# Key norms by statistics of two heads at a time, routing unrolled and staggered, self attention scored in quarters of the array

## The chip, the cores and the metric

The kernel runs on 1 core of one Trainium2 chip. The metric is the device time of one execution in microseconds (us), as the median of several runs. The hand-written program sets the order of work on each engine: TensorE (PE, with its weight loads PEld), VectorE (DVE), ScalarE (ACT), GpSimd (POOL) and SyncE (SP, whose queue issues DMAs). Engines meet at semaphores only.

## The reference

2,048 rows x of width 256 (64 batches of 32) go through six residual steps, each on layer-normed rows, with float32 throughout:

```
x = x + cross attention 0(norm(x), ctx)        16 heads, ctx 64 x 257 x 128
x = x + self attention(norm(x))                16 heads of 16, within each batch of 32 rows
x = x + experts(norm(x))                       64 experts, 8 of them per row, 64 places each
x = x + cross attention 1(norm(x), ctx)        16 heads of 128, RMS norm of queries and keys
x = x + self attention in fp4 weights(norm(x))
x = x + dense experts(norm(x))                 8 experts, 2 weighted
```

The change touches the second and third step, and a part of the fourth that is computed early. That part is the norm of the keys: for each of 16,448 context rows and each of 16 heads, 1/sqrt(mean of the 128 squared keys + 1e-5), where keys = ctx @ Wk:

```
k = (encoder_hidden_states @ Wk).reshape(B, Skv, H, D)
var = jnp.mean(jnp.square(k), axis=-1, keepdims=True);  rsqrt(var + EPS)
```

The third step gives each row its 8 best experts. An expert takes the first 64 rows that chose it (CAP = 64); what comes later goes nowhere and adds zero:

```
pos = (jnp.cumsum(onehot, axis=0) * onehot).sum(-1) - 1
dest = jnp.where(pos < CAP, slot_expert * CAP + pos, E * CAP)
slot_out = yb[dest] * topk_w      # row E * CAP of yb is zero
```

16,384 choices meet 64 x 64 = 4,096 places.

## The kernel before

x lies in SBUF as 16 tiles of 128 rows (NT = 16). Stages follow each other with a full meeting of all engines between them (`block`): begin, cross_attention 0, self_attention (prefix sa), route (rt), experts (ex), combine (cb), cross_attention 1, self_attention_fp4, dense_experts.

**Key norms** (class KeyNorms, used by rt, ex and cb with their own prefix). The context stands transposed in ctxT, 128 x 16,448: 128 chunks of 128 columns and a rest of 64. A chunk times Wk (128 x 2048) gives four PSUM banks of 512 keys (`keys`, L231, matmul L236; four heads to a bank). Three of the four are squared by ACT into SBUF (L268) and summed per head by DVE (tensor_reduce L295); the fourth is done by ACT alone, four squares with accumulation (L264). Every group of four chunks ACT takes roots (take_root, L275), DVE inverts (L303), PE turns (L243), DVE keeps (L309), and a DMA writes four copies to rk in DRAM. POOL copies the group's piece of ctxT to a staging tile first (put, L225), which the matmuls read. Chunks are shared out as rt 64 (4 a tile), ex 16, cb 48 and the rest.

**self_attention** (L915) is pipelined over tiles, two to a loop turn. Per tile PE turns xn (L972), projects queries and keys (L980) and values (L987), scores (L995), mixes (L1005) and projects out (L1012). k_heads holds the keys masked per head by POOL (L1206), so a score matmul gives 128 queries against 4 heads x 128 keys (all four batches of the tile against each other), four matmuls of 512 columns, though only the 32 x 32 blocks on the diagonal count. ACT picks those (keep_blocks, own_scores, L907, four pieces), DVE subtracts the maximum (L1132, L1133), ACT takes exp (L1074), DVE sums and divides (L1137, L1139) and transposes the blocks in four pieces into probsT (L1144). DVE adds the bias (L1148) and the result (L1150) to x. The mix waits until the add of the tile before is done, since out and mix share a PSUM bank.

**route** (L1224) is a loop of 8 turns of two tiles. Within a tile n PE does keys(0), logits (L1296), keys(1), keys(2), then waits until DVE has chosen the 8 best (L1365 to L1369), counts places (L1303, L1304), keys(3), the turning of the next tile's xn (L1285) and the group's norms (L243). DVE makes codes and places (L1379 to L1387) and the weights (8 operations at L1391, one per choice). POOL scatters the tile's rows with 8 indirect DMAs to slot_rows in DRAM (L1430). The router, Wk and the zeroing of slot_rows are DMAs at the start of the stage.

**experts** (L1437) takes two experts to a turn, 32 turns: rows turned (L1517), gate and up (L1526), hidden turned (L1533), out (L1540); stages lag by 1 and 2 turns. It has two banks for key norms (banks=2) and a chunk in every second turn. A turn's rows and weights come by four DMAs into a ring of 8, the first issued at the stage's start.

**combine** (L1614) takes a tile and a head to a turn, 16 turns in two loop turns of 8. POOL copies the tile's 8 places (L1771) and gathers with 8 indirect DMAs of 128 rows x 1 KB from slot_out (L1776) into one of two buffers got; DVE adds them with their weights (L1746). In between PE folds one head of cross attention 1's weights (turn_head L1668 to L1670, fold_head L1677, L1678; they wait for a load of Wq, Wv and Wo, issued at the start of the stage) and does three chunks of key norms.

```
                    for step, (j, slot, c) in enumerate(chunks(i, t)):
                        norms.keys(pe, j, slot, c)
                        if c == norms.U - 1:
                            norms.turn(pe, j)
                        if step == 0:
                            turn_head(h, t)
                    fold_head(h, t)
```

## Time and profile before

| | |
|---|---|
| median of 3 runs | 3160.76 us (3156.6 to 3161.11) |
| the profiled execution, its own time | 3129.82 us |
| its span on the core | 3128.2 us |
| mean granted TensorE clock | 0.965 |
| busy: PE / DVE / ACT / POOL | 90% / 51% / 46% / 24% |
| self_attention, span's us | 580.66 to 804.95 |
| route | 804.95 to 1121.06 |
| experts | 1121.06 to 1266.77 |
| combine | 1266.77 to 1536.19 |

The stages' limits are the times at which engines leave the meeting between two blocks. A stage's row of windows gives its length, the busy time of each engine in it, PE's mean granted clock and the DMA engines' busy share. PE's sum of busy times counts overlapping matmuls twice, so the starts of matmuls on the timeline tell more of a period than the busy share does.

### The profile page before, as it was taken

What the parts mean: (1) busy time and instruction counts of PE and PEld (TensorE: products, weight loads), DVE (VectorE), ACT (ScalarE), POOL (GpSimd) and SP (SyncE); (2) the same over time, 40 slices, a digit from 0 to 9 for tenths busy, and PEclk for the clock granted to TensorE, in tenths of its full rate; (3) what the DMA queues carried; (4) which work ended last, traced back from release to release, by engine and by line L of the source; (5) the groups of instructions that cost most, each with busy time, mean ns of one, the idle gap of its engine ahead of it and who ended that gap; (6) DMA issues with size and microseconds to landing.
All of it is one profiled execution on the core that took longest, in us unless ns stands there. A gap on an engine that the chain in (4) does not pass through costs nothing. (4 is left out here: it accounts for less than half of the span.)

```text
span 3128.2 us, 53136 instructions
## 1 busy us (share of the span) xinstructions
PE 2826.5 (90%) x13847; PEld 2100.0 (67%) x13847; DVE 1585.7 (51%) x4931; ACT 1436.8 (46%) x4275; POOL 738.0 (24%) x966
## 2 busy tenths in 40 slices
PE   6999999799788869689799999999589999997999
PEld 5888888676443434244367777777478888885888
DVE  3665556467577745477455555555123333332333
ACT  2555455444577756366355555554122223221333
POOL 1332223233345421465221112221310000000000
PEclk8999999899899989799899999999789999998999
DMA  4100000000210066467322222222730000000000
GB/s 150 29 27 23 20 23 13 16 0 0 99 34 7 7 162 192 132 77 74 52 75 74 74 74 74 74 65 63 169 76 0 0 0 0 0 0 27 7 10 10
DMA packets 174812, 157.10 MB, mean 50 GB/s; under 512 B 30315, under 2 KB 158184, under 8 KB 173570
## 3 DMA queue, kind: packets, MB, share of 16 engines
q1 hardware_dynamic: 153922, 130.12, 15.1%
q0 software_dynamic: 13824, 25.23, 5.3%
q10 hardware_dynamic: 6976, 0.75, 0.2%
q8 instruction: 32, 0.52, 0.1%
q14 instruction: 58, 0.48, 0.1%
HBM read 136.89 MB, written 31.67 MB: 54 GB/s over the span
## 5 line engine op out<-in xcount | busy, mean ns | idle before, releaser
L480 PE MATMUL xa_score_ps<-cross_ctxT,xa_qT 128*128 (+1 forms) x1024 | 307.9, 387 | 7.4 <-DVE xa_shift L724 4.1
L500 PE MATMUL xa_mix_ps<-xa_probsT,xa_keys 128*128 128x256 f32 x1024 | 304.2, 380 | 0.0
L236 PE MATMUL rt_kn_key_ps<-moe_wk,rt_kn_stage 128*128 128x512 f32 x512 | 238.7, 608 | 35.4 <-ACT rt_kn_squares L268 18.1
L470 PE MATMUL xa_misc_ps<-xa_xnT,cross_folded 128*128 128x256 f32 x1024 | 234.0, 383 | 6.2 <-ACT xa_squares L593 5.6
L509 PE MATMUL xa_misc_ps<-cross_folded,xa_mixT 128*128 128x256 f32 x1024 | 228.2, 379 | 0.0
L616 ACT ACTIVATE xa_probsT<-xa_probsT_ps 128x256 f32<-128x256 f32 x512 | 188.0, 369 | 79.4 <-PE xa_probsT_ps L487 78.9
L470 PEld LDWEIGHTS xa_misc_ps<-xa_xnT,cross_folded 128*128 128x128 f32 x1024 | 195.6, 192 | 40.0 <-ACT xa_squares L593 12.2
L487 PE MATMUL xa_probsT_ps<-all_ident,xa_probs 128*128 128x128 f32 x1024 | 198.4, 275 | 19.4 <-ACT xa_probsT L616 11.2
L509 PEld LDWEIGHTS xa_misc_ps<-cross_folded,xa_mixT 128*128 128x128 f32 x1024 | 194.6, 190 | 26.5
L236 PE MATMUL cb_kn_key_ps<-moe_wk,cb_kn_stage 128*128 128x512 f32 (+1 forms) x392 | 189.7, 633 | 22.1 <-POOL cb_kn_stage L225 10.2
L736 DVE TENSOR_SCALAR xa_probs<-xa_probs,xa_share 128x257 f32<-128x257 f32 x512 | 199.1, 389 | 18.2
L500 PEld LDWEIGHTS xa_mix_ps<-xa_probsT,xa_keys 128*128 128x128 f32 x1024 | 189.5, 190 | 24.0
L608 ACT ACTIVATE xa_probs<-xa_probs,xa_shift,xa_row_scale 128x257 f32<-128x257 f32 x256 | 153.7, 600 | 108.2 <-DVE xa_shift L724 103.0
L236 PEld LDWEIGHTS rt_kn_key_ps<-moe_wk,rt_kn_stage 128*128 128x128 f32 x512 | 92.3, 191 | 150.0 <-issue 85.6
L487 PEld LDWEIGHTS xa_probsT_ps<-all_ident,xa_probs 128*128 128x128 f32 x1024 | 133.6, 141 | 87.4 <-DVE xa_probs L736 27.9
L608 ACT ACTIVATE xa_probs<-xa_probs,xa_top 128x257 f32<-128x257 f32 x256 | 130.0, 508 | 106.9 <-DVE xa_top L720 104.9
L480 PEld LDWEIGHTS xa_score_ps<-cross_ctxT,xa_qT 128*128 128x128 f32 x1024 | 158.9, 190 | 22.6 <-DVE xa_shift L724 12.5
L907 ACT ACTIVATE sa_blocks<-sa_score_ps 32x512 f32<-32x512 f32 x128 | 75.3, 589 | 192.8 <-PE sa_score_ps L1909 149.4
L1885 PE MATMUL sa_work_ps<-sa_xnT,sa_wq 128*128 128x128 f32 x1024 | 130.3, 282 | 35.5 <-ACT sa_xnT L1955 13.4
L1430 POOL DMA_INDIRECT slot_rows<-rt_xn,rt_places x128 | 127.0, 992 | 141.7 <-DVE rt_places L1387 101.9
L236 PEld LDWEIGHTS cb_kn_key_ps<-moe_wk,cb_kn_stage 128*128 128x128 f32 (+1 forms) x392 | 76.6, 202 | 112.0 <-issue 84.2
L700 DVE COPY xa_qT<-xa_misc_ps 128x512 f32<-128x512 f32 x64 | 44.3, 692 | 207.0 <-PE xa_misc_ps L470 207.0
(316 smaller groups left out, 5750.6 us busy)
## 6 DMA issues: line engine op xcount, KB each, us to landing
xa_key_scale<-rk SPq DMA_DIRECT2D x256, 128.5 KB, 2.6
xa_rows<-in_ctx_dram SPq DMA_DIRECT2D x64, 128.0 KB, 2.1
xa_last_key<-in_ctx_dram SPq DMA_DIRECT2D x128, 64.0 KB, 2.9
xa_keys<-in_ctx_dram SPq DMA_DIRECT2D x64, 128.0 KB, 2.2
ex_w_in<-in_L_ffn_w_gate_dram SPq DMA_DIRECT2D x32, 192.0 KB, 3.4
ex_w_in<-in_L_ffn_w_up_dram SPq DMA_DIRECT2D x32, 192.0 KB, 3.7
ex_w_out<-in_L_ffn_w_down_dram SPq DMA_DIRECT2D x32, 192.0 KB, 4.1
slot_rows<-rt_zeros SPq DMA_DIRECT2D x4, 1024.0 KB
```

The source lines that it names most:

```text
L236: pe.matmul(self.key_ps[q % self.banks][0:n, :], self.stage[:, slot, u * P:u * P + n], self.wk[:, q * 512:(q + 1) * 512], start=True, stop ...
L470: ins = pe.matmul(misc_ps[hp % 2][:, j * N:(j + 1) * N], folded[:, 2 * hp + j, c * P:(c + 1) * P], xnT[:, c, :], start=(c == 0), stop=(c = ...
L480: pe.matmul(score_ps[s % 2][:, 0:S2], qT[:, b, r * HR:(r + 1) * HR, :].rearrange("p h t -> p (h t)"), ctxT[:, bass.ds((i * NB + b) * S2, S ...
L487: ins = pe.transpose(probsT_ps[s % 2][:, k * P:(k + 1) * P], probs[:, s % SR, k * P:(k + 1) * P], ident[:, :])
L500: ins = pe.matmul(mix_ps[b % 2][:, cols], keys[:, b % RING, k, :], probsT[:, b % 2, k, cols], start=(k == 0), stop=(k == KB - 1))
L509: ins = pe.matmul(misc_ps[t][:, 0:D], mixT[:, h, t * P:(t + 1) * P], folded[:, h, NC * P:FOLDED], start=(h == 0), stop=(h == H - 1))
L608: act.activation(probs[:, s % SR, :], probs[:, s % SR, :], ACT.Exp, bias=least, scale=scale, accum_out=total[:, col]).then_inc(exped, 1)
L616: act.activation(probsT[:, b % 2, :, r * P:(r + 1) * P], probsT_ps[s % 2][:, 0:KB * P].rearrange("p (k n) -> p k n", k=KB), ACT.Copy).then ...
L736: dve.tensor_scalar(probs[:, s % SR, :], probs[:, s % SR, :], share[:, col], None, ALU.mult).then_inc(probs_ready, 1)
L907: return act.activation(blocks[q, :, :], score_ps[q, :, q], ACT.Copy)
L1430: pool.indirect_dma_start(out=slot_rows, out_offset=bass.IndirectOffsetOnAxis(ap=places[:, u, k:k + 1], axis=0), in_=xn[:, u, :], in_offse ...
L1885: ins = pe.matmul(ps[:, j, :], w[:, c, h * HD:(h + 1) * HD], xnT[:, c, :], start=(c == 0), stop=(c == NC - 1))
```

## The change

- **Key norms.** The matmuls read ctxT itself. Banks 0 and 2 of a chunk go to DVE, which takes statistics straight from PSUM (`stat`): two bn_stats of 256 keys, the two heads interleaved by the access pattern, so that the even and the odd counts of one instruction are the two heads. Banks 1 and 3 go to ACT, four squares each with accumulation, in place in PSUM (`square`). Statistics become sums (`add_up`), and sums become roots, many chunks in one instruction. The roots of route's 64 chunks are taken at the start of experts (four, of 16 chunks), those of experts' chunks in combine.
- **Shares.** rt 64 as before, ex 32 (one each turn, still two banks), cb 33, among them the rest; two a tile.
- **Unrolled.** The loops of route, experts and combine are written out; indices are constants.
- **Route** is staggered: tile n-1 is counted, placed, weighed and scattered while tile n is turned, scored and chosen. xn has a ring of 4.
- **Loads.** Wk, router and the zeroing of slot_rows go into self_attention; the first 8 turns' expert weights are loaded during route, into `folded`, which is idle then.
- **Combine** gathers by slots_all directly, without the copy of places.
- **Self attention.** Scores are 8 matmuls [32 queries of a batch] x [8 heads x 32 keys], each batch in its quarter of the array's columns, into two alternating PSUM banks. keep_blocks is gone; DVE reads PSUM. The four transposes become one into flips (128 x 512), and ACT spreads it in four copies (`spread`). The bias is added by POOL. out has its own bank.

The diff, cut to its core:

```diff
+    def keys(self, pe, c):
+        n = self.rows(c)
+        for q in range(self.NQ):
+            m = self.order[c] * self.NQ + q
+            if m >= self.banks:
+                pe.wait_ge(self.act_took if q % 2 else self.dve_took, (m - self.banks) // 2 + 1)
+            pe.matmul(self.key_ps[m % self.banks][0:n, :], self.ctxT[:, c * P:c * P + n], self.wk[:, q * 512:(q + 1) * 512],
+                      start=True, stop=True).then_inc(self.keyed, 1)
...
+    def square(self, act, c):
+        n = self.rows(c)
+        for q in range(1, self.NQ, 2):
+            m = self.order[c] * self.NQ + q
+            act.wait_ge(self.keyed, m + 1)
+            for h in range(self.HQ):
+                keys = self.key_ps[m % self.banks][0:n, h * HD:(h + 1) * HD]
+                ins = act.activation(keys, keys, ACT.Square, accum_out=self.sums[0:n, c, q * self.HQ + h:q * self.HQ + h + 1])
+            ins.then_inc(self.act_took, 1)
...
+    def stat(self, dve, c, q):
+        n, m = self.rows(c), self.order[c] * self.NQ + q
+        dve.wait_ge(self.keyed, m + 1)
+        for p in range(self.HQ // self.PAIR):
+            heads = slice(p * self.PAIR * HD, (p + 1) * self.PAIR * HD)
+            ins = dve.bn_stats(self.stats[0:n, c - self.first, q // 2, p, :],
+                               self.key_ps[m % self.banks][0:n, heads].rearrange("p (h d) -> p d h", h=self.PAIR))
+        ins.then_inc(self.dve_took, 1)
...
-    def keys(self, pe, j, slot, u, n=P):
-        if u == 0:
-            pe.wait_ge(self.staged, j + 1)
-        for q in range(self.NQ):
-            pe.wait_ge(self.squared, j * self.PER + (u * self.NQ + q + 1))
-            pe.matmul(self.key_ps[q % self.banks][0:n, :], self.stage[:, slot, u * P:u * P + n], self.wk[:, q * 512:(q + 1) * 512],
-                      start=True, stop=True).then_inc(self.keyed, 1)
...
-            if self.on_act(u, q):
-                for h in range(self.HQ):
-                    col = slice(h * HD, (h + 1) * HD)
-                    ins = act.activation(squares[:, col], keys[:, col], ACT.Square,
-                                         accum_out=self.sums[0:n, slot, u, q * self.HQ + h:q * self.HQ + h + 1])
-                ins.then_inc(self.squared, 1)
-            else:
-                act.activation(squares, keys, ACT.Square).then_inc(self.squared, 1)
...
-            dve.tensor_reduce(self.sums[0:n, slot, u, q * self.HQ:(q + 1) * self.HQ],
-                              self.squares[0:n, q % self.SQ, :].rearrange("p (h d) -> p h d", h=self.HQ), AX_X, ALU.add
-                              ).then_inc(self.summed, 1)
...
+        score_ps = [sc.ps(f"score{n}", [P, AH, T]) for n in range(2)]
+        turn_ps, qk_ps, v_ps, mix_ps, out_ps = sc.ps("turn"), sc.ps("qk"), sc.ps("v"), sc.ps("mix"), sc.ps("out")
...
+            sp.dma_start(wk_next[:, :], I["L1_xattn_Wk"]).then_inc(ahead_loaded, 16)
+            sp.dma_start(router[:, :], I["L0_ffn_router_w"]).then_inc(ahead_loaded, 16)
+            zeros = x_sb[:, NT:, :].rearrange("p a d -> p (a d)")
+            for part in slot_rows.rearrange("(n p r) d -> n p (r d)", p=P, r=2):
+                sp.dma_start(part, zeros).then_inc(cleared, 16)
...
-                pe.wait_ge(blocks_kept, BT * n)
-                for m in range(AH // 4):
-                    ins = pe.matmul(score_ps[:, 4 * m:4 * m + 4, :], qkT[:, odd, m * 4 // HC, :],
-                                    k_heads[:, odd, 4 * m:4 * m + 4, :], start=True, stop=True)
-                ins.then_inc(scored, 1)
+                if not isinstance(n, int) or n > 1:
+                    pe.wait_ge(shifted, n - 1)
+                for c in range(NC):
+                    for b in range(BT):
+                        q = slice(b * T, (b + 1) * T)
+                        pe.matmul(score_ps[odd][q, c * HC:(c + 1) * HC, :], qkT[:, odd, c, q],
+                                  k_heads[:, odd, c * HC:(c + 1) * HC, q], start=True, stop=True).then_inc(scored, 1)
...
+            def spread(n, odd):
+                act.wait_ge(flipped, n + 1)
+                if not isinstance(n, int) or n > 1:
+                    act.wait_ge(mixed, n - 1)
                 for b in range(BT):
...
+                    q = slice(b * T, (b + 1) * T)
+                    act.activation(probsT[q, odd, :, q], flips[q, :, :], ACT.Copy).then_inc(probsT_ready, 1)
...
-                for b in range(BT):
-                    q = slice(b * T, (b + 1) * T)
-                    ins = dve.transpose(probsT[q, odd, :, q], blocks[q, :, :])
-                ins.then_inc(probsT_ready, 1)
-            def add(n, link):
-                link(dve.tensor_tensor(tile_of(n), tile_of(n), bias_out[:, :], ALU.add))
...
+                dve.wait_ge(probsT_ready, BT * n)
+                dve.transpose(flips[:, :, :], blocks[:, odd, :, :]).then_inc(flipped, 1)
...
+            def add_bias(n):
+                pool.wait_ge(normed, n + 1)
+                apart(pool, passed)
+                pool.tensor_tensor(tile_of(n), tile_of(n), bias_out[:, :], ALU.add).then_inc(based, 1)
...
+            for n in range(NT):
+                norms.keys(pe, PER * n)
+                turn_x(n)
+                norms.keys(pe, PER * n + 1)
+                logits(n)
+                if n:
+                    count(n - 1)
+                norms.keys(pe, PER * n + 2)
+                norms.keys(pe, PER * n + 3)
...
+        norms = norms_of(sc, range(ROUTED, ROUTED + TURNS), banks=2, spans=[(a, a + SPAN) for a in range(0, ROUTED, SPAN)],
+                         groups=[(a, a + 4) for a in range(0, ROUTED, 4)])
...
+            for t in range(TURNS + 2):
+                if t + 1 < TURNS:
+                    turn(t + 1)
+                if t < TURNS:
+                    middle(t)
+                    norms.keys(pe, ROUTED + t)
+                if 1 <= t <= TURNS:
+                    turn_hidden(t - 1)
+                if t >= 2:
+                    finish(t - 2)
+                j = group_of(t)
+                if j is not None:
+                    norms.turn(pe, j)
...
+            for k in range(ROUTED // SPAN):
+                norms.root(act, k, from_act=False)
+            for t in range(TURNS):
...
+        DONE = NT * 4 + E0 // 2
...
+        order = [LAST] + list(range(DONE, LAST))
+        spans = [(NT * 4, NT * 4 + 16), (NT * 4 + 16, DONE), (LAST, CHUNKS)] + [(a, a + 4) for a in range(DONE, LAST, 4)]
+        groups = [(a, a + 4) for a in range(NT * 4, DONE, 4)] + [(LAST, CHUNKS)] + [(a, a + 4) for a in range(DONE, LAST, 4)]
...
+            norms.keys(pe, LAST)
+            for t in range(NT):
+                norms.keys(pe, DONE + 2 * t)
+                if t == 0:
+                    pe.wait_ge(ahead_loaded, 48)
+                turn_head(t)
+                norms.keys(pe, DONE + 2 * t + 1)
+                norms.turn(pe, t)
+                fold_head(t)
+            norms.turn(pe, NT)
...
+            for t in range(NT):
+                if t >= U:
+                    pool.wait_ge(added, (t - U + 1) * K0)
+                apart(pool, passed)
+                for k in range(K0):
+                    pool.indirect_dma_start(out=got[:, t % U, k, :], out_offset=None, in_=slot_out,
+                                            in_offset=bass.IndirectOffsetOnAxis(ap=slots_all[:, t, k:k + 1], axis=0),
+                                            bounds_check=SLOTS, oob_is_err=False).then_inc(gathered[t % U], 16)
```

How the order of instructions moves, first PE in self_attention's loop body, one tile (before):

```order
L980 MATMUL sa_qk_ps<-sa_xnT,sa_wT 128x128 x8
L991 ISA
L993 REGISTER_ALU
L995 MATMUL sa_score_ps<-sa_k_heads,sa_qkT 128x512 x4
L969 REGISTER_ALU
L972 MATMUL sa_turn_ps<-all_ident,sa_xn 128x128 x2
L1005 MATMUL sa_mix_ps<-sa_probsT,sa_v_heads 128x128 x16
L987 MATMUL sa_v_ps<-sa_wT,sa_xnT 128x256 x2
L1012 MATMUL sa_mix_ps<-sa_outT,sa_mixT 128x256 x2
```

and after the change:

```order
L992 MATMUL sa_qk_ps<-sa_xnT,sa_wT 128x128 x8
L1003 ISA
L1010 MATMUL sa_score_ps<-cross_folded,sa_qkT 32x256 x8
L981 REGISTER_ALU
L984 MATMUL sa_turn_ps<-all_ident,sa_xn 128x128 x2
L1014 ISA
L1018 MATMUL sa_mix_ps<-cross_folded,sa_v_heads 128x128 x16
L999 MATMUL sa_v_ps<-sa_wT,sa_xnT 128x256 x2
L1026 MATMUL sa_out_ps<-sa_outT,sa_mixT 128x256 x2
```

The order is the same; the score is 8 matmuls of 32 x 256 in place of 4 of 128 x 512 (rows x columns of what they write). Next DVE in route, around the places of a tile, before:

```order
L1348 TENSOR_SCALAR rt_xn<-all_x,rt_mv,rt_rstd 128x256
L1379 TENSOR_TENSOR rt_code<-rt_slot_base,rt_place_ps 128x64
L1380 TENSOR_TENSOR rt_before<-rt_before,rt_chosen 128x64
L1381 SCALAR_TENSOR_TENSOR rt_picked<-rt_place_ps,rt_chosen 128x64
L46 REGISTER_ALU
L1383 TENSOR_TENSOR rt_code<-rt_code,rt_picked 128x64
```

and after (L265 is `stat`, two statistics to a bank):

```order
L265 BN_STATS moe_kn_stats<-rt_kn_key_ps 128x6 x2
L1399 SCALAR_TENSOR_TENSOR rt_picked,moe_weights<-rt_code,rt_codes,rt_gate 128x64 x8
L265 BN_STATS moe_kn_stats<-rt_kn_key_ps 128x6 x2
L1361 TENSOR_SCALAR rt_xn<-all_x,rt_mv,rt_rstd 128x256
L265 BN_STATS moe_kn_stats<-rt_kn_key_ps 128x6 x2
L1371 RECIPROCAL rt_scale<-rt_scale 128x1
L1372 TENSOR_SCALAR rt_prob<-rt_prob,rt_scale 128x64
```

The weights of tile n-1 now stand ahead of the choosing of tile n, with statistics between them, two instructions to each bank that PE waits to refill. Last PE in experts, a turn with a chunk and one without, before:

```order
L236 MATMUL ex_kn_key_ps<-moe_wk,ex_kn_stage 128x512 x4
L1517 MATMUL ex_turn_ps<-all_ident,ex_rows 128x128 x2
L1526 MATMUL ex_mid_ps<-ex_w_in,ex_rowsT 64x192 x4
L1533 MATMUL ex_hidden_ps<-all_ident,ex_hidden 96x128
L1540 MATMUL ex_out_ps<-ex_w_out,ex_hiddenT 64x256 x2
L1517 MATMUL ex_turn_ps<-all_ident,ex_rows 128x128 x2
L1526 MATMUL ex_mid_ps<-ex_w_in,ex_rowsT 64x192 x4
```

and after, one turn of those that also turn a group of norms:

```order
L1546 MATMUL ex_turn_ps<-all_ident,ex_rows 128x128 x2
L1558 MATMUL ex_mid_ps<-cross_folded,ex_rowsT 64x192 x4
L216 MATMUL ex_kn_key_ps<-moe_w_wk,cross_ctxT 128x512 x4
L1566 MATMUL ex_hidden_ps<-all_ident,ex_hidden 96x128
L1574 MATMUL ex_out_ps<-moe_in_w_out,ex_hiddenT 64x256 x2
L226 MATMUL ex_kn_rk_ps<-all_ident,moe_kn_sums 16x128 x4
```

Every turn now has the four key matmuls, between gate and up and the hidden rows of the turn before.

## Rows read from the trace of the kernel before

**Rows 1.** Windows, the four stages: start:end, length, busy time and count by engine, granted clock, DMA share, GB/s.

```profile
580.66:804.95 224.29, 188.60 (x1074) 142.94 (x1074) 147.09 (x231) 90.06 (x217) 75.90 (x72) 0.95 0.02 6
804.95:1121.06 316.11, 260.81 (x740) 121.03 (x740) 228.45 (x822) 225.49 (x802) 153.23 (x186) 0.97 0.14 37
1121.06:1266.77 145.71, 126.89 (x626) 59.76 (x626) 63.33 (x161) 86.26 (x265) 21.08 (x41) 0.93 0.66 192
1266.77:1536.19 269.42, 216.63 (x608) 102.17 (x608) 172.79 (x337) 152.85 (x573) 142.17 (x158) 0.90 0.61 89
```

**Rows 2.** Timeline of PE in self_attention: start, us, line, operation, what it waited for.

```profile
696.70 3.60 PE L995 MATMUL sa_score_ps<-sa_k_heads,sa_qkT 128*128 128x512 f32 x8
700.14 0.38 PE L972 MATMUL sa_turn_ps<-all_ident,sa_xn 128*128 128x128 f32 x2
```

**Rows 3.** All score matmuls of self_attention: count, ns min/median/max, first and last start.

```profile
L995 PE MATMUL sa_score_ps<-sa_k_heads,sa_qkT x128: 592/592/697, 602.3 to 782.4; 128*128 128x512 f32 x128
```

**Rows 4.** Timeline of PE, one turn of experts without a chunk and one with.

```profile
1185.37 0.51 PE L1517 MATMUL ex_turn_ps<-all_ident,ex_rows 128*128 128x128 f32 x2
1185.81 0.88 PE L1526 MATMUL ex_mid_ps<-ex_w_in,ex_rowsT 128*64 128x192 f32 x8
1186.62 0.31 PE L1533 MATMUL ex_hidden_ps<-all_ident,ex_hidden 128*96 128x128 f32 x1
...
1187.44 3.80 PE L236 MATMUL ex_kn_key_ps<-moe_wk,ex_kn_stage 128*128 128x512 f32 x8
1191.08 0.39 PE L1517 MATMUL ex_turn_ps<-all_ident,ex_rows 128*128 128x128 f32 x2
```

**Rows 5.** Timeline of PE in route, from the turning of one tile's xn to the next.

```profile
939.52 0.38 PE L1285 MATMUL rt_turn_ps<-all_ident,rt_xn 128*128 128x128 f32 x2
...
944.82 0.56 PE L1296 MATMUL rt_logit_ps<-rt_routerT,rt_xnT 128*128 128x64 f32 x4
945.21 3.65 PE L236 MATMUL rt_kn_key_ps<-moe_wk,rt_kn_stage 128*128 128x512 f32 x8
950.83 3.70 PE L236 MATMUL rt_kn_key_ps<-moe_wk,rt_kn_stage 128*128 128x512 f32 x8 [1.97 <-ACT rt_kn_squares L268]
...
958.52 0.38 PE L1285 MATMUL rt_turn_ps<-all_ident,rt_xn 128*128 128x128 f32 x2
```

**Rows 6.** Groups of instructions, 830 to 1110 us (busy, mean ns, idle before).

```profile
L1430 POOL DMA_INDIRECT slot_rows<-rt_xn,rt_places x124 | 123.1, 993 | 140.4 <-DVE rt_places L1387 101.9 <-issue 38.3 <-DVE rt_mv L895 0.3
L295 DVE TENSOR_REDUCE cross_sums<-rt_kn_squares 128x4 f32<-128x512 f32 x185 | 116.7, 678 | 7.9 <-ACT rt_kn_squares L268 4.2 <-issue 1.8
```

**Rows 7.** Timelines: PE at the start of route; POOL at its end; PE at the start of experts.

```profile
812.77 0.69 PE L1285 MATMUL rt_turn_ps<-all_ident,rt_xn 128*128 128x128 f32 x2 [5.25 <-DMA moe_wk<-in_L_xattn_Wk_dram]
...
1115.02 0.97 POOL L1430 DMA_INDIRECT slot_rows<-rt_xn,rt_places  x1 [0.30 <-issue]
...
1127.63 0.70 PE L1517 MATMUL ex_turn_ps<-all_ident,ex_rows 128*128 128x128 f32 x2 [19.14 <-DMA ex_w_out<-in_L_ffn_w_down_dram]
```

**Rows 8.** Timelines: ACT's squares, DVE's statistics of 256 columns, a strided copy.

```profile
945.28 0.33 ACT L264 ACTIVATE rt_kn_squares<-rt_kn_key_ps 128x128 f32<-128x128 f32 x1
...
945.53 0.34 ACT L264 ACTIVATE rt_kn_squares<-rt_kn_key_ps 128x128 f32<-128x128 f32 x1
...
1536.32 0.75 DVE L677 BATCH_NORM_STATS2 xa_stats<-all_x 128x6 f32<-128x256 f32 x2 [5.83 <-PEq L81]
...
1539.39 0.21 DVE L799 COPY xa_last_ctx<-cross_ctxT 128x64 f32<-128x64 f32 x1
```

**Rows 9.** Timelines in combine: POOL's gathers, PE's first turn_head.

```profile
1473.95 1.00 POOL L1776 DMA_INDIRECT cb_got<-slot_out,cb_places  x1 [0.30 <-issue]
...
1288.33 0.69 PE L1668 MATMUL cb_turned_ps<-all_ident,cross_wq 128*128 128x128 f32 x2 [13.87 <-DMA cb_wo<-in_L_xattn_Wo_dram]
```

**Rows 10.** Windows within combine (columns as in rows 1).

```profile
1306.00:1330.00 24.00, 20.86 (x60) 9.76 (x59) 16.29 (x34) 13.29 (x49) 17.27 (x18) 0.97 0.36 100
1452.00:1482.00 30.00, 26.88 (x78) 12.86 (x77) 22.20 (x43) 18.75 (x76) 18.09 (x21) 0.94 0.98 85
```

933 lines of the change are left out of this document (453 added, 480 removed).

## The prediction

> **What bounds the kernel now.** I read the windows of the four stages first [rows 1]: which engine is busiest, and at what clock; then the timeline of PE inside each stage, since the starts of its matmuls give the true period; then groups and timelines for the price of single operations. The profiled execution took 3129.82 us against a median of 3160.76, 31 us or 1.0% less. I sum against the profiled one and carry the difference over to the median; 1% of a change of some tens of us is nothing. What lies outside 580.66 to 1536.19 is not touched and stays.
>
> Self attention (224.3 us) is bound by PE: a score takes 3.44 us from its start to the next matmul [rows 2], and 15 periods lie between the first and the last tile's scores, 11.8 us each (the last record starts at 782.4, its tile some 3 us before) [rows 3]. Route (316.1 us) has a period of 19.0 us at the tile shown [rows 5], and PE waits in it: 1.97 us on ACT for the squares, ahead of that some more. DVE's reduces alone are 0.63 us x 12 a tile [rows 6]. Experts takes 2.07 us for a turn without a chunk and 3.64 more with one (start to start) [rows 4]. Combine is bound by three things in turn: a weight load to +21.6 us [rows 9], then the issue of gathers on POOL, then, late, DMA at a share of 0.98 [rows 10].
>
> **Self attention: -40.** A score is 8 records of 512 columns, 0.43 us each [rows 2]. After it is 16 records of 256, 0.215 each if they followed each other, which is the same 3.44; it only gains where the four column quarters run beside each other. The nearest row: gate and up are 8 records of 192 columns whose two experts stand in two halves of the columns. At 0.16 a record they would take 1.29 us, and they take 0.81 start to start [rows 4], so halves do overlap. The ends: no overlap, 3.4 us; full overlap of four, 0.86. I take 1.1, which is nearer to the full one as the row shows 1.6 of 2. That is 2.3 x 15 = -35 in the loop. The wait chain of a tile (score, maximum, exp, sum, transpose, spread, mix) loses ACT's four pieces and gains four others, off PE's path. POOL takes the bias beside work. The tail after the last score loses some 5. The loads added run at a DMA share of 0.02 [rows 1]: nothing. The Trainium skill, "TensorEngine Tiling (Array Packing)", section "Theoretical Speedup", gives up to 4x for a small dimension of up to 32; by its best case alone the loop would gain 2.6 x 15 = 39 (an estimate); the rows show less than the full factor for halves.
>
> **Route: -51.** PE per tile after: 16 banks of two records of 512 columns, 0.43 each as in [rows 2] = 13.7, turn 0.2, logits 0.4 (944.82 to 945.21) [rows 5], counts, as many records again with a wait, 0.6: 14.9. DVE: its busy time of 228.5 less 192 reduces of 0.63 leaves 107 for 16 tiles, 6.7 each [rows 1, 6], of which 1.2 (inverse and keeping) goes to experts. Gaps in its chain add some 1.5. To that come 16 statistics. On SBUF two of 256 columns take 0.75 [rows 8], 0.35 to 0.37 in sequence. So DVE: 5.5 + 1.5 + 16 x 0.36 = 12.8. ACT: 8 banks x 4 squares x 0.25 [rows 8] = 8.0, exp and xnT 0.9, no table loads: 9. POOL: 8 scatters x 1.27 [rows 7] = 10.2. PE bounds at 15.1 with a little for the ring of four banks, and 16 x 15.1 = 241.6. The start loses its DMA waits (PE's first turn was at +7.7 [rows 7]): 3. The last tile's choosing, counting and placing, then 8 scatters of 1.27, stand exposed with the meeting: 20. 265 against 316.
>
> **Experts: +76.** Every turn has a chunk, in two banks. Bank 2 waits until DVE has two statistics of bank 0 (0.75), bank 3 until ACT has four squares of bank 1 (1.0, before it stands in ACT's queue silu): 4.0 us a chunk for 3.64 before. 32 x (2.07 + 4.0) = 194. Turning the norms of route, four transposes of 0.15 in 16 turns: 10. The start, 7: PE's first matmul was 19.1 us after its last work of route, on the DMA of the last of four loads [rows 7]; now weights are there and only rows come, but four roots and two table loads stand in ACT's queue ahead of the first silu. Tail 11. 222 against 145.7. This is the cost of 16 chunks moved in: 64 of the 76.
>
> **Combine: -41.** PE has two chunks for three: 6.8 + 0.4 + 1.0 + 0.4 = 8.7 us a tile; DVE 4 banks x 0.75, 8 adds of some 0.5, and 1.8 for inverses, sums and the turned head's copies: 8.7. Gathers: a pitch of 1.30 on POOL [rows 9], so 8 x 1.30 + 0.3 = 10.7 a tile. The window late in the stage shows 85 GB/s at a DMA share of 0.98 against 100 at 0.36 early [rows 10]: almost all choices of late tiles are NOWHERE, so their gathers read one row of DRAM. About 7 GB/s of the 85 are the norms' copies (6 chunks x 32 KB in 30 us), so a gather of 131 KB takes 131/78 = 1.7 us, 13.7 a tile, and that the change does not touch. So: 21.6 until Wo is there [rows 9], tile 0 and the half of 1 to the first add at +38, four tiles of 10.7 to +81, ten of 13.8 to +219, landing, adds and meeting 9: 228 against 269. The removed copy of places (0.2 and its waits) is in the 0.3.
>
> **The sum:** -40 - 51 + 76 - 41 = -56: profiled 3074, median 3160.8 - 56 = **3105**.
>
> **Rivals.** *The statistics read PSUM with a stride (slower).* Each read jumps 128 floats between the two heads. No row shows statistics of PSUM or with a stride. Bounds: 0.36 from SBUF [rows 8] and, if each element cost twice, 0.15 + 2 x 0.27 = 0.68, where 0.27 is 256 columns at the pitch of these rows. A strided copy of 64 columns in SBUF takes 0.21 [rows 8], no more than a plain one, which speaks for 0.36. At 0.68 DVE's tile in route is 7.0 + 10.9 = 17.9, over PE's 15.1: +2.8 x 16 = +45. In experts bank 2 waits 0.6 longer and bank 0 of the next turn a little: +30. Combine keeps its DMA bound. +75: 3180, **slower by 19**. It decides from about 0.61 us an operation. The Trainium skill, "Advanced Engine Details and Errata", section "PSUM Cachelines", says that PSUM's lines hold two float32 and that patterns which are not contiguous slow down matmuls; whether statistics too, no run here shows, and by it the time would be this rival's. 15%.
>
> *The quarters do not overlap* (the change does not do what it says): the score stays at 3.4, self attention gains the 5 of the tail: 3140. Against it speaks the 0.81 of [rows 4], for it that this row has halves only. 11%.
>
> *Late gathers are not bound by one row* but by how POOL issues them beside other work: combine at 10.7 for all tiles, -30 more: 3075. For it: POOL was busy 18.09 of 30 us late and 17.27 of 24 early [rows 10], so issue is not far off. 12%.
>
> *Written-out loops:* no jump back, so stalls of several us at the two turns of combine and the eight of route go; or more instructions are to be fetched than DMAs bring in time. Either way some 10, within the range.
>
> **How the numbers follow.** Main case 52% (3090 to 3120), statistics 15%, no overlap 11%, gathers 12%, a mix of small losses (experts' turn at 6.8 for 6.1, +22, with half an overlap) 7%, near 3145, statistics and overlap both bad 3%, over 3190. The range has to leave out no more than 2 in 10: 3062 to 3168 leaves out the statistics case, mixes beyond it and a few lucky ones. A measurement here can tell 0.2%, 6 us, from no change. Faster by more: 52 + 11 + 12 + 3 = 78%. Within 0.2%: 5%, a mild statistics case. Slower: 17%.
>
> **What would show it.** Windows of the four stages after: 184, 265, 222 and 228 us. In self attention the score's start to start at 1.1; if 3.4, the quarters fail. In route the statistics' pitch at 0.36 and PE without waits on DVE; if PE waits for DVE's statistics, it is the first rival. In experts chunk to chunk 6.1 us. In combine gathers end last and DMA's share is over 0.9 from tile 6 on. The prediction is wrong if experts grows less than 60 (then bank waits are shorter than I think, or DMA did bind before), or if combine does not shrink, since then something other than PE's chunks set it.

## The result: slower, and where the time went

The change makes the kernel **1% slower**: 3189.93 us (median of 4 runs, 3186.38 to 3194.85) against 3159.82 for the kernel before, measured beside it, ratio 1.0098, 95% interval 1.008 to 1.0115. Forecast was 3105, with 3168 as the upper end. The profiled execution after took 3186.38 us, span 3184.6, clock 0.948.

Windows of the changed kernel, one for each stage, in the columns of [rows 1]; self attention, route, experts, combine, and then the cross attention of layer 1, whose code the change does not touch. Three of them begin up to 1.2 us beside the stage's first instruction: that of self attention stands at 578.99, of experts at 1023.72, of combine at 1327.12.

```profile
580.00:749.80 169.80, 150.77 (x1202) 126.70 (x1202) 111.80 (x167) 91.75 (x217) 90.85 (x84) 0.93 0.11 39
749.80:1022.50 272.70, 243.41 (x674) 114.09 (x674) 180.00 (x849) 166.11 (x1073) 140.10 (x165) 0.96 0.13 34
1022.50:1326.90 304.40, 230.37 (x800) 93.83 (x800) 83.11 (x249) 105.83 (x598) 17.36 (x32) 0.84 0.27 82
1326.90:1572.06 245.16, 170.37 (x489) 79.75 (x489) 130.37 (x333) 99.39 (x573) 130.10 (x128) 0.85 0.73 99
1572.06:2267.37 695.31, 647.25 (x2848) 482.70 (x2848) 356.77 (x1441) 340.89 (x937) 129.10 (x225) 0.98 0.24 67
```

From first instruction to first instruction, as in [rows 1], self attention lost 53.5 us (forecast -40), route 42.2 (-51), combine 24.5 (-41). Experts grew by 157.7, where +76 was forecast. The last row is the surprise outside the change: the same stage took 677.4 us before (1536.19 to 2213.6), so +17.9.

**Self attention.** All score matmuls, then PE's timeline over a tile (start, us, operation, what it waited for):

```profile
L1010 PE MATMUL sa_score_ps<-cross_folded,sa_qkT x256: 379/379/489, 601.5 to 732.0; 128*32 128x256 f32 x128
```

```profile
698.16 1.07 PE L1010 MATMUL sa_score_ps<-cross_folded,sa_qkT 128*32 128x256 f32 x16
699.16 0.44 PE L984 MATMUL sa_turn_ps<-all_ident,sa_xn 128*128 128x128 f32 x2
```

Sixteen records of 256 columns take 1.00 us start to start, for 3.44 in [rows 2]: the quarters do run beside each other. (The Trainium skill, "TensorEngine Tiling (Array Packing)", section "Theoretical Speedup", gives up to 4x; the trace has 3.4.) The tile's period is (732.0 - 601.5) / 15 = 8.7 for 11.8. Of the 3.1 won, 2.4 is the score; the rest goes with waits of PE that are gone. The largest is the one for DVE's xn ahead of the turn: 11.8 us in all before (600 to 800 us), 1.8 after (600 to 748). It stood in some of the tiles of before:

```profile
689.16 0.44 PE L972 MATMUL sa_turn_ps<-all_ident,sa_xn 128*128 128x128 f32 x2 [1.70 <-DVE sa_xn L1128]
```

**Route.** The changed kernel's timeline of PE, and all statistics on PSUM (count, ns min/median/max, first and last start):

```profile
893.53 0.38 PE L1291 MATMUL rt_turn_ps<-all_ident,rt_xn 128*128 128x128 f32 x2
893.75 2.74 PE L216 MATMUL rt_kn_key_ps<-moe_w_wk,cross_ctxT 128*128 128x512 f32 x6
897.28 1.13 PE L216 MATMUL rt_kn_key_ps<-moe_w_wk,cross_ctxT 128*128 128x512 f32 x2 [0.78 <-remote]
899.08 9.23 PE L216 MATMUL rt_kn_key_ps<-moe_w_wk,cross_ctxT 128*128 128x512 f32 x21
```

```profile
L265 DVE BATCH_NORM_STATS2 moe_kn_stats<-rt_kn_key_ps x256: 399/415/433, 752.6 to 997.4; 128x6 f32<-128x256 f32 x128
```

One statistic takes 0.415 us and a pair in sequence 0.75 (the ordinary row reads `0.75 DVE L265 ... x2`), as on SBUF in [rows 8]. The stride in PSUM costs nothing here, and PE waits only 4.9 us ahead of its key matmuls from 752 to 1020 us. The first rival has fallen: what the Trainium skill says of matmuls in "Advanced Engine Details and Errata", section "PSUM Cachelines", does not carry over to statistics here.

**Experts.** Groups, 1030 to 1320 us (busy, mean ns | idle before, what ended it):

```profile
L216 PE MATMUL ex_kn_key_ps<-moe_w_wk,cross_ctxT 128*128 128x512 f32 x256 | 157.8, 736 | 60.8 <-DVE moe_kn_stats L265 57.8 <-ACT ex_kn_key_ps L237 3.0
L256 ACT ACTIVATE ex_kn_rkT<-ex_kn_rk_ps 16x512 f32<-16x512 f32 x16 | 9.4, 586 | 75.7 <-DMA rk<-ex_kn_rkT 75.7
```

PE waits 60.8 us ahead of the chunks, for DVE. That is the symptom: DVE works 83 of 304 us. ACT's row tells more: its 16 copies of turned norms wait 75.7 us in all, for a **store**. One turn, in the timelines of SP (its queue), ACT and PE:

```profile
1066.56 0.37 SPq L1480 DMA_DIRECT2D cross_folded<-in_L_ffn_w_gate_dram  x1
1066.97 1.25 SPq L1480 DMA_DIRECT2D cross_folded<-in_L_ffn_w_up_dram  x1
1068.27 0.47 SPq L1481 DMA_DIRECT2D moe_in_w_out<-in_L_ffn_w_down_dram  x1
1068.78 0.47 SPq L1524 DMA_DIRECT2D ex_rows<-slot_rows  x1
1069.29 0.72 SPq L301 DMA_DIRECT2D rk<-ex_kn_rkT  x1
```

```profile
1072.67 0.59 ACT L256 ACTIVATE ex_kn_rkT<-ex_kn_rk_ps 16x512 f32<-16x512 f32 x1 [5.60 <-DMA rk<-ex_kn_rkT]
1073.17 0.36 ACT L1598 ACTIVATE ex_rowsT<-ex_turn_ps 128x256 f32<-128x256 f32 x1
1073.43 0.22 ACT L1605 ACTIVATE ex_gate<-ex_mid_ps 128x96 f32<-128x96 f32 x1
```

```profile
1067.22 0.88 PE L1558 MATMUL ex_mid_ps<-cross_folded,ex_rowsT 128*64 128x192 f32 x8
1068.03 1.98 PE L216 MATMUL ex_kn_key_ps<-moe_w_wk,cross_ctxT 128*128 128x512 f32 x4
1074.74 3.56 PE L216 MATMUL ex_kn_key_ps<-moe_w_wk,cross_ctxT 128*128 128x512 f32 x4 [4.72 <-DVE moe_kn_stats L265]
1079.36 0.40 PE L1546 MATMUL ex_turn_ps<-all_ident,ex_rows 128*128 128x128 f32 x2
```

`rkT` is a ring of two. `keep(j)` waits until the store of group j-2 has landed, and SP issues that store only once a turn's output is made, behind three weight loads and the rows, 2.7 us after the first of them. ACT stands until 1072.67; behind it in its queue are the rows' copy and the sigmoid's input. DVE multiplies after those, and takes the chunk's statistics after that; PE needs them for its third bank. Then PE finishes the turn, SP may go on, and the ring closes: 12.4 us a turn, 14 turns from 1066.9 to 1240.9. Where no groups are kept any more, turns from 1240.91 on take 6.3 us (1247.47 for the next), with 6.1 forecast. 14 x (12.4 - 6.3) = 85, which is the whole excess of 82 over the forecast. PE's granted clock goes with its waiting: 0.78 in the 14 long turns, 0.99 in the short ones up to 1300.

**Combine and cross attention 1** are read beside the experiments on them, below.

### The profile page after: what moved, and what is told of

Its sections match the earlier page's. It is cut to its first block and busy times, and to the rows that moved or that the text cites. A ratio compares the mean times of both kernels' runs of the same rounds, so it can differ in the third digit from the quotient of the medians.

```text
span 3184.6 us, 50492 instructions
## 1 busy us (share of the span) xinstructions
PE 2833.8 (89%) x13964; PEld 2089.7 (66%) x13964; DVE 1477.4 (46%) x4978; ACT 1344.6 (42%) x4879; POOL 722.9 (23%) x924
## 5 line engine op out<-in xcount | busy, mean ns | idle before, releaser
L216 PE MATMUL rt_kn_key_ps<-moe_w_wk,cross_ctxT 128*128 128x512 f32 x512 | 231.2, 600 | 5.3 <-remote 4.5
L216 PE MATMUL ex_kn_key_ps<-moe_w_wk,cross_ctxT 128*128 128x512 f32 x256 | 157.8, 736 | 60.8 <-DVE moe_kn_stats L265 57.8
L733 DVE TENSOR_SCALAR xa_probs<-xa_probs,xa_share 128x257 f32<-128x257 f32 x512 | 198.2, 387 | 18.2
L216 PE MATMUL cb_kn_key_ps<-moe_w_wk,cross_ctxT 128*128 128x512 f32 (+1 forms) x264 | 141.8, 678 | 36.4 <-issue 11.8
L216 PEld LDWEIGHTS rt_kn_key_ps<-moe_w_wk,cross_ctxT 128*128 128x128 f32 x512 | 94.3, 191 | 117.5 <-issue 98.5
L237 ACT ACTIVATE rt_kn_key_ps<-rt_kn_key_ps 128x128 f32<-128x128 f32 x512 | 135.5, 265 | 77.0 <-PE rt_kn_key_ps L216 58.1
L1817 POOL DMA_INDIRECT cb_got<-slot_out,moe_slots x128 | 130.1, 1016 | 106.2 <-issue 55.5
```

The source lines that it names most:

```text
L216: pe.matmul(self.key_ps[m % self.banks][0:n, :], self.ctxT[:, c * P:c * P + n], self.wk[:, q * 512:(q + 1) * 512], start=True, stop=True). ...
L237: ins = act.activation(keys, keys, ACT.Square, accum_out=self.sums[0:n, c, q * self.HQ + h:q * self.HQ + h + 1])
L733: dve.tensor_scalar(probs[:, s % SR, :], probs[:, s % SR, :], share[:, col], None, ALU.mult).then_inc(probs_ready, 1)
L1817: pool.indirect_dma_start(out=got[:, t % U, k, :], out_offset=None, in_=slot_out, in_offset=bass.IndirectOffsetOnAxis(ap=slots_all[:, t, k ...
```

## The experiments

Totals of the kernel before differ by chip: 3157 us on the first here (e1, e2, e3, e5), 3132 on the second (e4, e6, e7, e8), 3096 on the third (e9 to e12), 3138 on the fourth (e13 to e15). Ratios compare only within a chip. Stages are read from one profile each, from the stage's first instruction on, but experts only from PE's first row turn to combine's first chunk (301.4 after, 140.2 before); in `rt` is all from route's start up to that turn.

| kernel | median us | ratio (95%) | rt | experts | combine | cross 1 |
|---|---|---|---|---|---|---|
| before (first profile) | | | 322.7 | 140.2 | 268.4 | 677.4 |
| e1 before again | 3158.22 | 1.0002 (0.9992, 1.0012) | 340.6 | 141.3 | 278.4 | 675.0 |
| the change | 3189.93 | 1.0098 (1.008, 1.0115) | 275.9 | 301.4 | 244.9 | 695.3 |
| e2 ring of 4 | 3106.46 | 0.9832 (0.9812, 0.9852) | 274.8 | 218.9 | 247.4 | 697.9 |
| e3 store first | 3109.74 | 0.9844 (0.9824, 0.9865) | 275.4 | 218.6 | 249.9 | 695.3 |
| e5 rows spread | 3158.89 | 1.0004 (0.9995, 1.0014) | 275.7 | 299.3 | 246.6 | 675.5 |
| e4 e2, 3 buffers | 3096.69 | 0.9874 (0.9839, 0.9909) | 268.0 | 218.7 | 243.2 | 696.7 |
| e6 e4, spread | 3080.21 | 0.9831 (0.9807, 0.9855) | 273.6 | 219.2 | 235.5 | 675.4 |
| e7 e2, 16 chunks back | 3033.13 | 0.9682 (0.9658, 0.9705) | 268.1 | 151.6 | 243.3 | 695.3 |
| e8 e2, 96 memsets | 3098.04 | 0.9888 (0.9864, 0.9911) | 268.1 | 218.8 | 242.9 | 691.0 |
| e9 e2, 60 memsets | 3067.23 | 0.9908 (0.9892, 0.9924) | 267.9 | 219.0 | 237.5 | 675.0 |
| e10 e7, 60 memsets | 3009.72 | 0.9718 (0.9705, 0.9731) | 267.9 | 152.0 | 244.0 | 676.1 |
| e11 e7, spread | 2996.92 | 0.9675 (0.9661, 0.969) | 273.1 | 151.6 | 223.4 | 676.4 |
| e12 e2, ACT copies | 3067.87 | 0.9907 (0.9892, 0.9922) | 267.8 | 218.9 | 236.7 | 674.4 |
| e13 e2 again | 3098.33 | 0.9878 (0.9859, 0.9897) | 269.1 | 218.6 | 243.3 | 696.6 |
| e15 e2, spread | 3074.54 | 0.9791 (0.9772, 0.981) | 274.9 | 218.6 | 233.5 | 676.8 |
| e14 e11, 3 buffers | 3016.47 | 0.9605 (0.9581, 0.9629) | 273.4 | 152.7 | 247.3 | 675.1 |

### The kernel before once more

No edit: is the first profile, 31 us under the median, the right one to subtract from?

> The kernel before, unchanged, for a profile beside the others. What differs in cross attention 1, whose code the change does not touch: before's profile had 677 us there, after's 695. Theory A (the place of the code): the loop body of cross attention 1 stays where it was, so no instruction is fetched again in each turn; its turns take 82.6 us and the stage 677 us, and the time is near 3160 all the same, so the 31 us between profile and median lie elsewhere. Theory B (a state of the chip or of the session): the stage takes 690 us or more here too, with turns near 85.5 us, and the change is not the cause.

3158.22 us, and this time the profiled execution was an ordinary one (span 3158.9). It took 18 us more than the first in route and 10 more in combine, and cross attention stayed at 675. So the first profile was a lucky one, in those two stages; with one ordinary profile to set against it, how often that happens is not known. Against e1, the change gives: self attention -53.5, route -64.7, experts +160.1, combine -33.4, cross attention +20.3, the rest -3.1: +25.7, the difference of the two spans.

### The ring of turned norms

```diff
-            self.rkT, self.rk_ps = sc.sb("kn_rkT", [H, 2, GROUP]), sc.ps("kn_rk")
+            self.rkT, self.rk_ps = sc.sb("kn_rkT", [H, keeps, GROUP]), sc.ps("kn_rk")
-        if j > 1:
-            act.wait_ge(self.rk_stored[j % 2], 16 * (j // 2))
+        if j >= keeps:
+            act.wait_ge(self.rk_stored[j % keeps], 16 * (j // keeps))
```

> The change with four buffers for the turned norms in experts instead of two. Theory A (a new wait: ACT keeps group j only when the store of group j-2 has landed, and SP issues that store behind three weight loads after the out matmul of the same turn): the 14 turns of 12.4 us fall to 6.3, experts from 304 to about 218 us, the total from 3190 to about 3105. Rival (two banks and PE's half clock make the turns long; the wait on the store only shows what would be lost anyway): experts stays over 280 us and the total over 3165. Rival 2 (weights come too late, the DMA behind binds): turns of 8 to 10 us, total 3130 to 3150.

And with two buffers, but SP's store moved ahead of the loads and two turns earlier:

```diff
                 sp.wait_ge(out_made, t + 1)
+                j = group_of(t + 2)
+                if j is not None:
+                    norms.store(sp, j)
                 loads(t + BUF, loaded[t % BUF])
                 load_rows(t + BUF)
-                j = group_of(t)
-                if j is not None:
-                    norms.store(sp, j)
```

> The change with two buffers as it is, but SP issues the store of a group two turns earlier in its own order, ahead of that turn's weight loads. By the theory of the late store this alone gives what four buffers give: experts near 218 us, total near 3105, within 5 us of the ring of four. If instead the number of buffers matters by itself (the store's own 3 us from issue to landing), it gains only part: turns of 8 to 9 us, total about 3140.

Both: 3106.46 and 3109.74 us, experts 218.9 and 218.6. Groups in experts of e2 (its file has one line more, so L217 is L216 of the change):

```profile
L217 PE MATMUL ex_kn_key_ps<-moe_w_wk,cross_ctxT 128*128 128x512 f32 x256 | 136.9, 638 | 5.7 <-ACT ex_kn_key_ps L238 5.5
L257 ACT ACTIVATE ex_kn_rkT<-ex_kn_rk_ps 16x512 f32<-16x512 f32 x16 | 9.4, 586 | 1.0
```

The 75.7 us of ACT are 1.0, and PE's 60.8 are 5.7. Two edits that share nothing but this wait give the same 83 us. The two banks and the weight loads are as they were in both, so neither rival of the expectation holds; the low clock went too (0.96 in e2's experts, 0.84 in the change's), so it was an effect of the waiting and not its cause. The cause of the miss in experts is **shown**.

### Chunks back to where they were

With the ring of four, experts takes its 16 chunks of before (every second turn), combine its three a tile.

```diff
-                    norms.keys(pe, ROUTED + t)
+                    if t % 2 == 0:
+                        norms.keys(pe, ROUTED + t // 2)
...
+        PER = 3
-                norms.keys(pe, DONE + 2 * t + 1)
+                norms.keys(pe, DONE + PER * t + 1)
+                norms.keys(pe, DONE + PER * t + 2)
```

> Four buffers, and the chunks of key norms shared out as before the change: 16 in experts, in every second turn, three a tile in combine. By the prediction's reading (a chunk costs 4 us of every turn in experts, and combine has the place under its gathers): experts 218 to about 155 us, combine 247 to at most 260, total 3106 to about 3045 to 3060. Rival (combine's PE and DVE have no place, each chunk costs what it takes): combine 247 + 16 x 3.4 = 300, total 3100. The roots come one a tile here, two table loads each, on ACT.

Experts 151.6 for 218.9, combine 243.3 for 247.4: ratio 0.9682. On the same chip e8, whose code is e2's with memsets, took 3098.04 us, 65 more. The prediction called the 16 chunks 64 of experts' 76; they cost 67. What they bought in combine has to be read where DVE's stalls, described below, don't blur it: e9 and e10 are e2 and e7 on one chip, without stalls, and there combine takes 237.5 with two chunks a tile and 244.0 with three. So 16 chunks fewer bought 6.5 us for 67. Rebalancing them was the wrong way round for this program.

### Combine: one row, two buffers, and stalls

The late gathers read almost only the one row of zeros. Here each partition has its own:

```diff
-        slot_out = nc.dram_tensor("slot_out", (SLOTS + 1, D), F32).ap()
+        slot_out = nc.dram_tensor("slot_out", (SLOTS + P, D), F32).ap()
```

(and a choice that is NOWHERE gets NOWHERE plus its partition's number).

> The change with 128 rows of zeros behind slot_out in place of one, each partition's empty choices gathered from its own row. Theory of the one row: late gathers are held back by reading one row of DRAM (packets of 0.74 us against 0.16 early); spread, DMA's share late in combine falls from 1.0 to under 0.5 and pairs of tiles fall from 24 to 27 us to what the early ones take or less, combine 245 to 225 to 235. Theory of two buffers: POOL issues 16 gathers in 20.9 us and then waits some 7 us for the adds of both, early as well as late, so combine stays within 5 us of 245 though DMA's share falls.

Windows late in combine, 1460 to 1550, of the change and then of e5:

```profile
1460.00:1550.00 90.00, 67.13 (x203) 31.96 (x201) 49.77 (x126) 40.44 (x236) 53.20 (x53) 0.92 0.94 85
```

```profile
1460.00:1550.00 90.00, 58.04 (x180) 28.70 (x179) 46.51 (x118) 35.56 (x207) 49.36 (x49) 0.83 0.30 80
```

DMA's share falls from 0.94 to 0.30: the row was what kept DMA busy. But combine stays at 246.6, as the theory of two buffers had it; e15 and e11, below, show that the row counts all the same. Of the 31 us that the kernel gains by its medians 20 are cross attention's; e5's profiled execution was 9 us over its median (3167.59), so its combine may be a long one. Then a third buffer for gathered rows, alone and with the spread rows, both with the ring of four:

```diff
-        U = 2
+        U = 3
```

> Four buffers for the turned norms (3106.5 by itself) and three for the gathered rows in combine instead of two (the turned weights take the place of sums that are no longer read). Theory of two buffers (POOL must wait for the adds of both tiles before it issues the next 16 gathers): combine falls from 247 us to 210 to 225, total 3070 to 3085. Theory of the one row (DMA at a share of 1.0 late): gathers take 13.7 us a tile whatever the buffers, combine stays over 238, total over 3097.

> As with four and three buffers, and the empty choices spread over 128 rows of zeros. If the one row binds as soon as the buffers don't, combine falls another 15 to 25 us, to some 200 (POOL issues 8 gathers in 10.5 us, 168 for all, and 30 at the ends); if not, it stays within 5 us of the run without spread rows. Cross attention 1, not touched: by the theory of the place of the code (spread rows put 96 more instructions on DVE ahead of its loop) 675 us here and 695 to 698 in the run without them.

243.2 and 235.5. Neither is what a clean theory gives. The reason stands in DVE's rows. Timeline of DVE in combine of the change, then the group of the first of these operations, 1330 to 1570:

```profile
1380.05 0.76 DVE L265 BATCH_NORM_STATS2 moe_kn_stats<-cb_kn_key_ps 128x6 f32<-128x256 f32 x2 [3.14 <-PE cb_kn_key_ps L216]
1385.79 0.48 DVE L1777 TENSOR_SCALAR cb_wT<-cb_turned_ps,cb_gain 128x256 f32<-128x256 f32 x1 [4.97 <-issue]
1386.19 0.41 DVE L1778 COPY cb_wT<-cb_turned_ps 128x256 f32<-128x256 f32 x1
1389.30 0.76 DVE L265 BATCH_NORM_STATS2 moe_kn_stats<-cb_kn_key_ps 128x6 f32<-128x256 f32 x2 [2.71 <-DMA in_wo<-in_L_xattn_Wo_dram]
```

```profile
L1777 DVE TENSOR_SCALAR cb_wT<-cb_turned_ps,cb_gain 128x256 f32<-128x256 f32 x16 | 7.7, 482 | 44.5 <-issue 29.7 <-remote 12.0 <-PE cb_turned_ps L1716 2.7
```

DVE stands for 5 us ahead of a copy whose inputs PE had made 7 us before (1377.66 to 1378.3), and 2.7 ahead of statistics whose keys are there; the Wo named as releaser is another stage's, whose last load was issued at 10.7 us. Of the 44.5 us ahead of the copies 14.0 are no such stall: the first copy (1350.31) waits for PE's first turned head, and that for this stage's weights. In the stretch shown POOL issues 16 gathers in one run (1368.46 to 1389.2). The longest stalls came ahead of statistics, 15.2 us in e4 and this one in e5, with PE waiting for DVE behind it; a few of them are enough to hide what a third buffer or spread rows bring:

```profile
1527.75 1.42 DVE L265 BATCH_NORM_STATS2 moe_kn_stats<-cb_kn_key_ps 128x6 f32<-128x256 f32 x4 [15.42 <-DMA in_wo<-in_L_xattn_Wo_dram]
1528.57 6.17 PE L216 MATMUL cb_kn_key_ps<-moe_w_wk,cross_ctxT 128*128 128x512 f32 x8 [12.06 <-DVE moe_kn_stats L265]
```

Does a place in the code, an operation of DVE, or the run itself make them? With the two copies on ACT:

```diff
-                dve.tensor_scalar(w[:, 0:2 * P], ps[:, 0:2 * P], gain[:, 0:1], None, ALU.mult)
-                dve.tensor_copy(w[:, 2 * P:4 * P], ps[:, 2 * P:4 * P]).then_inc(wT_ready, 1)
+                act.activation(w[:, 0:2 * P], ps[:, 0:2 * P], ACT.Copy, scale=gain[:, 0:1])
+                act.activation(w[:, 2 * P:4 * P], ps[:, 2 * P:4 * P], ACT.Copy).then_inc(wT_ready, 1)
```

> The change with four rkT buffers, and the two copies that keep a turned head in combine are made by ACT instead of DVE. With two chunks a tile DVE stands still ahead of these copies for 45 us of combine in all, while nothing that they wait for is late, and POOL issues gathers one behind the other. Theory, that just these two copies of DVE are held up while POOL issues: the stalls ahead of them go, combine falls from 247 us to 232 or less, ratio about 0.978. Rival, that any instruction of DVE is held up then, or that the gathers themselves set the end: the waits move to the statistics or to the adds, combine stays at 243 to 248. Cross attention 1 stays at 691 to 698 us (its DVE loop begins at 107).

Combine 236.7. But e9, on the same chip with the copies on DVE, has 237.5 and no stalls either, so e12 tells nothing of them; and its DVE loop lay at 92, not at 107 as I wrote, so its cross attention took 674.4 us. Then e2's code again, on a fourth chip:

> The kernel e2 once more (the change with four rkT buffers), for combine. There DVE stood still ahead of the copies of the turned heads for 45 us in all and POOL issued its gathers sixteen in one run; in e9, the same code with 60 memsets ahead of it, these stalls are gone, POOL issues eight at a time, DVE waits for gathers and combine takes 237.5 us for 247.4. Theory, that this too hangs on the place of DVE's code: the stalls are there again, combine at 245 to 249 us. Rival, that it is a state of the chip or of the run into which the same code can fall or not: no stalls and combine at 236 to 239 us. In both cases experts takes 219 us and cross attention 1 695 to 698.

243.3: stalls up to 1376 (5.1, 6.3, 4.2, 3.5, 4.2 and 4.3 us among them), none in the 107 us behind. The same code has them for most of combine (e2), for a part of it, and e9, which differs in memsets alone, not at all. So they are not a fixed property of the code. Nor is a long run of gathers enough: in e9 POOL issues 40 of them in one run, 1281.84 to 1335.2, and from the first adds to the end of combine DVE has no wait of 1.5 us or more for anything but PE or a gather. So the gathers without a pause may as well follow from the stalls, which let two buffers come free together. What the stalls are is **open**.

What e9 shows without them is what the prediction meant to describe. Groups of DVE in its combine (L1790 are the adds):

```profile
L1790 DVE SCALAR_TENSOR_TENSOR all_x<-cb_got,moe_weights,all_x 128x256 f32<-128x256 f32 x128 | 60.9, 476 | 73.3 <-DMA cb_got<-slot_out,moe_slots 69.9
L1781 DVE TENSOR_SCALAR cb_wT<-cb_turned_ps,cb_gain 128x256 f32<-128x256 f32 x16 | 7.7, 478 | 16.8 <-PE cb_turned_ps L1718 16.6
```

Gathers end the waits. From combine's start its first adds come at +35.5, tile 4's at +77.1, tile 15's at +230.3: 11 late tiles of 13.9 us, and the end at +237.5. With the spread rows and e7's chunks:

> The kernel e7 with one row of zeros for each of the 128 partitions, so that the late gathers of combine do not all read one row; its 64 more instructions on DVE put the loop body of cross attention 1 at 85. In e7 a tile of combine took 12.1 us early and 13.5 late, with DVE waiting for gathers; that spreading the rows made nothing alone (e5) I lay to DVE's stalls in combine with two chunks a tile, which e7 does not show. Theory: late tiles fall to about 12.1, combine by 8 to 12 us, cross attention 1 at 675 to 678, ratio 0.957 to 0.960. Rival, that the late tiles are not bound by the one row: combine as in e7 (243 us), ratio 0.961 to 0.963 by the place alone.

Combine 223.4, ratio 0.9675. Windows of e7 and then e11, both 1290 to 1380:

```profile
1290.00:1380.00 90.00, 83.08 (x253) 39.86 (x251) 62.68 (x162) 57.38 (x345) 50.04 (x49) 1.00 0.98 87
```

```profile
1290.00:1380.00 90.00, 90.00 (x282) 44.79 (x281) 72.18 (x191) 63.75 (x383) 58.92 (x59) 1.00 0.35 97
```

DMA 0.98 becomes 0.35, and PE is busy all the time: the one row was the bound, and PE is the next, at 12.06 us from one tile's turned head to the next. Against e10, on the same chip and also without stalls, combine gains 20.6 us, twice what I expected, but the kernel only 12.8 (3009.72 to 2996.92): the spread choices take more instructions in route, and `rt` is 5.2 us longer. The ratios that I expected for e9 to e12 all came out 0.007 to 0.013 too high, since on this chip the kernel before is 36 to 61 us faster than on the others; it has no profile here that could say where.

> Four rkT buffers and one row of zeros for each partition. In e5 the rows were spread and combine stayed at 246.6 us, with DVE's stalls; in e11, without such stalls, spreading took 20 us from combine. If the stalls are there as in e5: combine 245 to 248 us, DMA below a share of 0.4 late in the stage. If they are not: tiles at about 12, combine 220 to 226. Cross attention 1 at 675 to 677 us in both (its DVE loop begins at 75).

> The kernel e11 (four rkT buffers, a chunk in every second turn of experts, three a tile in combine, spread rows; combine 223.4 us, ratio 0.9675 on its chip) with three buffers for gathered rows in place of two. In e11 POOL waits 44.7 us of combine for adds before it may gather into a buffer again, and PE is busy for 202 of the 223. Theory, that the two buffers are next in line: combine falls by 6 to 15 us, ratio 0.963 to 0.966. Rival, that PE's three chunks or DVE's adds set the tile: combine 221 to 225, ratio 0.967 to 0.968.

e15 has combine at 233.5, between its two cases, with stalls up to 9 us; that is 10 less than e13 on the same chip. e14 has 247.3 in its profile, 24 more than e11 and outside both of its cases, with a stall of 10.6 us and others. Its runs spread from 3003 to 3028, and against e13 on the same chip it stands at 3016.47 / 3098.33 = 0.974, or 0.980 without the 20 us (0.007) of cross attention, while e11 against e9, with nothing of these in it, stands at 0.977. A third buffer brings nothing sure, and my theory for it is not borne out.

### Cross attention 1: the place of a loop

> Four buffers, and 96 one-element memsets on DVE at the start of combine, where it waits for weights anyway; nothing else. Theory of the place of the code: cross attention 1 falls from 698 to about 675 us, its DVE loses the wait of 2.9 us in each turn of the loop and no instructions are fetched in the loop; total 3106 to about 3086. If cross attention 1 stays at 695 or more, its loss has another cause (what spread rows changed in data or DMAs).

> The change with four rkT buffers (as the run e2, in which cross attention 1 took 697.9 us), and 60 one-element memsets on DVE at the start of combine. Nothing in cross attention is touched. In the runs so far the loop of that stage took 675 to 677 us where DVE's loop body began 65, 75 or 104 instructions past a multiple of 128, and 691 to 698 where it began 11, 21 or 106 past one; 96 memsets had moved it from 11 to 106 and changed nothing. With 60 it begins at 71. Theory of place: cross attention 1 at 675 to 678 us, with some 10 instruction packets in place of 40, and the kernel about 20 us under e2's ratio, 0.976 to 0.979. Rival, that what the stage before leaves behind in the queues makes the difference: 691 to 698 us and a ratio of 0.983.

```diff
             norms.invert(dve, 0, 1)
             dve.wait_ge(gain_ready, 1)
+            for n in range(60):
+                dve.memset(filler[:, n:n + 1], 0.0)
```

> The kernel e7 (four rkT buffers, a chunk in every second turn of experts, three a tile in combine; ratio 0.968, cross attention 1 at 695.2 us) with the same 60 memsets, which move DVE's loop body of cross attention 1 from 21 to 81 past a multiple of 128. Theory of place: 675 to 678 us there, ratio 0.961 to 0.963. Rival: 695 us and 0.968.

DVE's timeline in the change, in the stage's loop; the group of this operation over the whole stage; and the instruction queue over one turn (1722 to 1808; packets, MB, share), which shows nothing for a turn of before:

```profile
1788.26 0.43 DVE L717 CUSTOM_DVE_ANT_0 xa_probs<-xa_score_ps,xa_key_scale 128x257 f32<-128x257 f32 x1 [2.88 <-issue]
```

```profile
L717 DVE CUSTOM_DVE_ANT_0 xa_probs<-xa_score_ps,xa_key_scale 128x257 f32<-128x257 f32 x256 | 108.0, 422 | 75.4 <-PE xa_score_ps L477 45.7 <-issue 22.0 <-DMA xa_key_scale<-rk 3.4
```

```profile
q14 instruction: 5, 0.04, 0.2%
```

Once a turn DVE waits 2.9 us with nothing late, 22.0 in the stage (`issue`). The other kernels whose stage takes 691 us or more have 18.2 to 23.4 there; where it takes 674 to 677, it is 1.2 at most among the waits named. And instructions are fetched again each turn, 40 packets in the stage for 10 before. The place of DVE's loop body (344 instructions), counted in its program modulo 128, against the stage's time:

```
before, e1         67    677.4, 675.0
the change, e2-e4  11    695.3 to 697.9   (e13: 696.6)
e7                 21    695.3
e9                 70    675.0
e5, e6, e15        75    675.5, 675.4, 676.8
e10                80    676.1
e11, e14           85    676.4, 675.1
e12                92    674.4
e8                106    691.0
```

(The expectation of e9 names a place 104 with a short stage; no kernel lies there. That of e6 speaks of 96 more instructions; there are 64, and it lies at 75.) With 60 useless memsets the stage takes 675.0 us for the 697.9 and 696.6 of e2's code; with 96, 691.0. Fetching each turn goes with it: 10 or 11 packets in the stages of 674 to 677 us, 40 or 41 in those of 691 to 698. **Shown** is that the long stage, DVE's wait of about 20 us and the fetching in each turn come and go together, in all profiles of the kernels listed, while the stage's code is the same; that DVE waits for those instructions is the natural reading of it. That the place decides is well supported and not quite shown. As first put, the theory failed: e8 was to take 675 us and took 691, and its place, 106, was then counted with 11 and 21. Since then it forecast e9, e10, e11 and e15 rightly, and e12 by its real place. One rival is left: the two kernels with memsets and a short stage ran on the third chip, on which no long stage was profiled, and on the other chips the changed kernels with a short stage are those with spread rows. No two runs on one chip differ in memsets alone and have one stage of each kind. Why those places, and whether 128 is the right modulus, is open too. And the memsets make no kernel faster that a ratio could show: 0.9908 and 0.9718 for e9 and e10 against 0.9832 and 0.9682 for e2 and e7, each on another chip.

## Why the prediction was wrong

**The failed step is experts' term, +76.** It priced a chunk (6.1 us a turn, measured 6.3), the start and the tail, and said of the norms that are turned there "four transposes of 0.15 in 16 turns: 10". It priced PE's part of a moved step and left out its other instructions: ACT's copy, with a wait on a ring of two, and SP's store, queued behind three weight loads. What stands behind a waiting instruction on its engine was not asked for that one. It cost 82 to 83 us: turns of 12.4 us where 6.1 was forecast, 14 times. The diff had it all, `if j > 1: act.wait_ge(...)` and the place of `norms.store` in SP's loop; a count of turns between a store's issue and the wait on it would have told. With that wait gone (e2), experts is 221 us (1025.7 to 1246.7), between the same limits as the forecast of 222. The whole miss, 3190 for 3105, adds up: experts 81.7 over, cross attention 17.9, combine 16.5, route 8.8, elsewhere 1.0, less 13.5 of self attention, less 27.4 that the prediction carried over from the lucky profile (30.9 us under its median, where the changed kernel's is 3.6 under).

**That e2 comes out at 3106, one us from the forecast, is luck in part.** Other terms missed and cancelled:

- Self attention: -40 forecast, -53.5 measured. The quarters overlap, as taken (1.0 for 1.1). The ends gave 7 us for 5. Missed was some 10 us of PE's waits in the loop, above all that for DVE's xn (11.8 to 1.8); that it went because a tile has less work on DVE (147.1 us of the stage to 111.8) is likely but no run took it apart.
- Route: -51 forecast, -42.2 measured against the profile used; with the start of experts in it, -46.8, and -64.7 against an ordinary run (e1). PE's tile is 15.3 us on average, with 15.1 forecast, its first turn comes at +5.8 for +3, and the tail took 23 for 20. The profile used was 18 us faster in this stage than the median's, and I carried the difference over as if it lay outside.
- Combine: -41 forecast (228 us), -24.5 measured. The late tiles are the 13.8 us forecast (e9: 13.9), and the one row is the cause, as said (e11). But 16 tiles have 15 periods, and the sum had four and ten: 14. The right sum is 38 + 4 x 10.7 + 11 x 13.8 + 9 = 242, and e9 took 237.5. The stalls of DVE took more: e2 has 10 us more than e9, which has none.
- Nothing was forecast for cross attention 1: "What lies outside 580.66 to 1536.19 is not touched and stays." Untouched it was; it took 18 us more.

**The rivals.** Strided statistics: refuted, 0.75 us a pair from PSUM. Quarters without overlap: refuted. Late gathers bound by issue: refuted, since tiles grow from 10.4 to 13.9 us in e9 with the same gathers to issue, and spreading the row is what moved them (e11), where no stalls hid it. Written-out loops, "some 10" either way and placed where the loops are: the cost of fetching came, 20 us, but in a loop that nobody had written out. The rival that did occur, a store late behind loads, was not among them.

**The signs named for it.** Neither "wrong if" came true: experts grew by more than 60, and combine shrank. Both looked for experts or combine moving less than forecast, none for experts growing too much. What did point at the place was the list of numbers ahead of them: 303.4 us where 222 was to stand, and 12.4 from chunk to chunk for 6.1.

## What to carry to other kernels

When a step moves to another stage, follow each of its instructions there, down to the DMA that frees its buffer: where in the issuing queue does it stand, behind what, and how many turns before the wait on it. A wait on a store must be as many turns behind as the queue is late; a ring of four instead of two was worth 83 us here. And work given to a stage with a busy engine should be taken from one that it really bounds: the 16 chunks cost 67 us in experts for 6.5 in combine, and e7 and e11 win 3% with the chunks where they were.

## What the runs showed that I had not expected

- A loop of 344 DVE instructions, itself unchanged, took 675 or 695 us for its stage: in the long case 2.9 us a turn of waiting, and five 8 KB packets of instructions fetched each turn. Both went together in every profile; what stood ahead of the loop in the program is the likely cause. After any edit it pays to look at untouched stages too.
- DVE can stand still for 2 to 15 us ahead of instructions whose inputs are there, in stretches in which POOL issues indirect gathers without a pause; but such stretches came without stalls too (e9), and neither the four kernels on the third chip nor e7 on the second had any. Some 10 us of combine hang on it (247.4 in e2, 237.5 in e9), and its cause is open.
- Gathers of many rows that are nearly all one row of DRAM kept DMA at a share of 0.94 to 0.98, with a packet of 4 KB at 0.77 us in the median (the change, e7); gathers from 128 rows in the same stretches, at 0.30 to 0.35 and 0.16 us (e5, e11).
- Statistics of a strided view of PSUM cost the same as plain ones of SBUF: 0.75 us for two of 256 columns.
